# Loading the attention weights by casting transfers and issuing every second FFN weight load from ScalarE

## The reference, cut to what matters

```python
x = x + attn(layernorm(x), Wq, bq, Wk, bk, Wv, bv, Wo, bo)
# ffn, on layernorm(x):
h = silu(tlin(x, w1_w, w1_s)) * tlin(x, w2_w, w2_s)      # 1024 -> 4096
h = gelu(tlin(h, h1_w, h1_s))                            # 4096 -> 4096
h = gelu(tlin(h, h2_w, h2_s))                            # 4096 -> 4096
return x_mid + tlin(h, w3_w, w3_s)                       # 4096 -> 1024
```

## Time and profile before

| | us |
|---|---|
| median of 2 runs | 6946.5 (6782.0 and 7111.1) |
| the profiled execution | 6785.2 |
| its span, slowest core | 6783.7 |
| spans of the 8 cores | 6731.2 to 6783.7 |
| TensorE busy | 5790.8 (85%) |
| VectorE, ScalarE, GpSimd busy | 959.4, 658.8, 389.6 |
| end of the attention part | about 1370 |

### The profile page before, as it was taken

One profiled execution on the slowest core, in us unless ns is written; L12 is line 12 of the kernel. 1 busy time (PEld: TensorE's weight loads), 2 busy tenths in 40 slices (PEclk: granted clock), 3 DMA queues, 4 the chain that ended last, 5 costly groups with the idle time before them and its releaser, 6 DMA issues.

```text
span 6783.7 us, 75111 instructions; the slowest of 8 cores (6731.2 to 6783.7 us)
## 1 busy us (share of the span) xinstructions
PE 5790.8 (85%) x28409; PEld 2752.3 (41%) x28409; DVE 959.4 (14%) x2378; ACT 658.8 (10%) x1088; POOL 389.6 (6%) x625
## 2 busy tenths in 40 slices
PE   0355558969997999799979998999899989998998
PEld 0233335534443444344434443444344434443444
DVE  0343336620002000200020002000200020002000
ACT  0000000011001100110011001100100010001100
POOL 0000001100000000000000000000000000000000
PEclk9977779989998999999999999999999999999999
DMA  9999971034443444344434433444344334443443
GB/s 160 129 124 125 125 107 38 35 109 149 149 149 127 152 149 157 124 149 154 155 124 149 151 147 124 149 150 148 128 151 148 144 130 149 149 143 124 152 152 137
DMA packets 143589, 919.33 MB, mean 136 GB/s; under 512 B 16064, under 2 KB 16128, under 8 KB 65808
## 3 DMA queue, kind: packets, MB, share of 16 engines
q0 software_dynamic: 83488, 536.50, 30.8%
q1 hardware_dynamic: 59760, 378.04, 16.1%
HBM read 974.76 MB, written 126.35 MB: 162 GB/s over the span
## 4 chain that ended last, share of the span: by engine, by line
PE 73%; DMA 10%; another core or an unknown queue 7%; DVE 4%; issue 4%; ACT 1%; DVEq 0%; POOL 0%; POOLq 0%; ACTq 0%; SPq 0%
PE Z L892 50%; DMA p_w12r<-w12s 7%; PE Z L932 6%; PE Z L830 4%; PE Z L844 3%; PE Z L598 3%; PE Z L661 2%; PE Z L633 2%; DMA p_wbig<-h1s 1%; PE Z L549 1%; DMA p_wbig<-h2s 1%; PE Z L796 0%; PE Z L441 0%; DVE f_lnfm L800 0%
## 5 line engine op out<-in xcount | busy, mean ns | idle before, releaser
L892 PE MATMUL Z<-f_aT,p_wbig 128*128 128x512 bf16 x8192 | 1780.5, 379 | 13.4 <-DMA p_wbig<-h1s 6.5
L892 PE MATMUL Z<-f_bT,p_wbig 128*128 128x512 bf16 x8192 | 1779.6, 379 | 9.7 <-DMA p_wbig<-h2s 6.2
L892 PEld LDWEIGHTS Z<-f_aT,p_wbig 128*128 128x128 bf16 x8192 | 796.2, 98 | 996.4 <-issue 47.6
L892 PEld LDWEIGHTS Z<-f_bT,p_wbig 128*128 128x128 bf16 x8192 | 796.9, 98 | 991.1 <-issue 41.2
L830 PE MATMUL Z<-f_lnfm,p_w12r 128*128 128x512 bf16 x2048 | 494.4, 385 | 161.1 <-DMA p_w12r<-w12s 160.3
L947 DVE TENSOR_SCALAR f_o3T<-Z,p_s 128x512 f32<-128x512 f32 x64 | 48.1, 751 | 3981.8 <-PE Z L932 3981.8
L844 PE MATMUL Z<-f_lnfm,p_w12r 128*128 128x512 bf16 x2048 | 489.7, 382 | 6.2 <-DVE f_ost L965 6.2
L932 PE MATMUL Z<-f_aT,p_wbig 128*128 128x512 bf16 x2048 | 446.0, 379 | 5.1 <-DMA p_wbig<-w3s 2.7
L598 PE MATMUL Z<-a_lnfm,a_wq 128*128 128x256 bf16 (+1 forms) x1088 | 148.9, 306 | 287.2 <-DVE a_wot L557 285.0
L830 PEld LDWEIGHTS Z<-f_lnfm,p_w12r 128*128 128x128 bf16 x2048 | 193.1, 98 | 438.0 <-issue 233.8
L912 ACT ACTIVATE f_aT<-Z,p_sh 128x512 bf16<-128x512 f32 x256 | 176.0, 687 | 1612.0 <-PE Z L892 1612.0
(11 more groups left out here) (89 smaller groups left out, 2198.3 us busy)
## 6 DMA issues: line engine op xcount, KB each, us to landing
p_wbig<-h1s SPq DMA_DIRECT2D x128, 1024.0 KB, 4.8
p_wbig<-h1s POOLq DMA_DIRECT2D x128, 1024.0 KB, 6.1
p_wbig<-h2s SPq DMA_DIRECT2D x128, 1024.0 KB, 4.8
p_wbig<-h2s POOLq DMA_DIRECT2D x128, 1024.0 KB, 5.8
p_w12r<-w12s POOLq DMA_DIRECT2D x135, 512.0 KB, 3.7
p_w12r<-w12s SPq DMA_DIRECT2D x121, 512.0 KB, 3.2
h1s<-h1b POOLq DMA_DIRECT2D x8, 4096.0 KB, 194.6
h2s<-h2b POOLq DMA_DIRECT2D x8, 4096.0 KB, 114.2
```

The costliest lines, as they stand in the source:

```text
L892: N0=N0: e.matmul(zb[:, 0:N0], wbig[ws][:, ic * 128:ic * 128 + 128], src[:, ic * TPMAX:ic * TPMAX + N0], start=(ic == 0), stop=(ic == NHC ...
```

## The change

Two edits. First, Wk, Wv and Wo are loaded as Wq is, by casting transfers that GpSimd issues; the staging buffer, the six conversions and the waits on `stg_done` go away. Second, the FFN weight loads that GpSimd issued (odd chunks, and both of `w12_pref`) are issued by ScalarE, at the same place in the list and with the same waits on buffers; they count on SyncE's pool of semaphores.

```diff
@@ start @@
     cast_w("wq", wq_s)
+    cast_w("wk", wk_s)
+    cast_w("wv", wv_s)
     load_x(2)
     load_x(3)
-    stg = ar.al("a_stg", [128, 4096], F32, at=ar.offset_of(xmst[0]))
-    prev_conv = None
-    cvi = 0
-    for nm, dst in (("wk", wk_s), ("wv", wv_s), ("wo", wo_s)):
-        evs = []
-        for h in range(2):
-            ld = E("sy", lambda e, s=w_in[nm], h=h: e.dma_start(
-                out=stg[:], in_=s[:, h * 4096:(h + 1) * 4096]),
-                waits=[prev_conv], inc=sd, inc_by=16)
-            if cvi % 2 == 0:
-                cv = E("dv", ... e.tensor_copy(...), waits=[ld], inc=dv)
-            else:
-                cv = E("ac", ... e.copy(...), waits=[ld], inc=ac)
-            cvi += 1
-            prev_conv = cv
-            evs.append(cv)
-        wcast[nm] = tuple(evs)
-    stg_done = prev_conv
+    cast_w("wo", wo_s)
@@ wo_tile @@
-                       wotmp_free[u % 2] if oh == 0 else None,
-                       stg_done if (u <= 1 and oh == 0) else None], inc=dv)
+                       wotmp_free[u % 2] if oh == 0 else None], inc=dv)
...
-                   xmid_spill[u - 2] if u >= 2 else None,
-                   stg_done if u <= 1 else None], inc=po)
+                   xmid_spill[u - 2] if u >= 2 else None], inc=po)
@@ ffn_stage_a @@
-                w12_pref[(p, sl)] = E("gp", lambda e, sl=sl: e.dma_start(
+                w12_pref[(p, sl)] = E("ac", lambda e, sl=sl: e.dma_start(
                     out=w12r[sl][:], in_=w12s[sl]),
                     waits=[conv_ev[("w12", 0)], w12_free[sl]],
-                    inc=gd, inc_by=16)
+                    inc=sd, inc_by=16)
@@ ffn_pass, w12 chunks @@
-                eng, pool = ("sy", sd) if oc % 2 == 0 else ("gp", gd)
+                eng = "sy" if oc % 2 == 0 else "ac"
                 d1 = E(eng, lambda e, oc=oc, sl=sl1: e.dma_start(
                     out=w12r[sl][:], in_=w12s[oc]),
                     waits=[conv_ev[("w12", oc // 8)], w12_free[sl1]],
-                    inc=pool, inc_by=16)
+                    inc=sd, inc_by=16)
@@ ffn_pass, h1 and h2 chunks @@
-                eng, pool = ("sy", sd) if pc % 2 == 0 else ("gp", gd)
+                eng = "sy" if pc % 2 == 0 else "ac"
                 dd = E(eng, lambda e, pc=pc, hs=hsrc, ws=wslot: e.dma_start(
                     out=wbig[ws][:], in_=hs[pc]),
                     waits=[conv_ev[(hkey, pc // 4)], wbig_free[wslot]],
-                    inc=pool, inc_by=16)
+                    inc=sd, inc_by=16)
```

More of the change, by code:

```diff
@@ L289, in build_nc @@
     cast_w("wq", wq_s)
+    cast_w("wk", wk_s)
+    cast_w("wv", wv_s)
     load_x(2)
     load_x(3)
-    stg = ar.al("a_stg", [128, 4096], F32, at=ar.offset_of(xmst[0]))
-    prev_conv = None
-    cvi = 0
-    for nm, dst in (("wk", wk_s), ("wv", wv_s), ("wo", wo_s)):
-        evs = []
-        for h in range(2):
-            ld = E("sy", lambda e, s=w_in[nm], h=h: e.dma_start(
-                out=stg[:], in_=s[:, h * 4096:(h + 1) * 4096]),
-                waits=[prev_conv], inc=sd, inc_by=16)
-            if cvi % 2 == 0:
-                cv = E("dv", lambda e, d=dst, h=h: e.tensor_copy(
-                    d[:, h * 4096:(h + 1) * 4096], stg[:]),
-                    waits=[ld], inc=dv)
-            else:
-                cv = E("ac", lambda e, d=dst, h=h: e.copy(
-                    d[:, h * 4096:(h + 1) * 4096], stg[:]),
-                    waits=[ld], inc=ac)
-            cvi += 1
-            prev_conv = cv
-            evs.append(cv)
-        wcast[nm] = tuple(evs)
-    stg_done = prev_conv
+    cast_w("wo", wo_s)
     ld_ev = {}
```

## The result

The changed kernel took 9952.0 us as the median of 11 runs (9576.6 to 10133.9), the kernel before 6948.1 us as the median of 10. The profiled execution took 9581 us with a span of 9579.5, against 6785 and 6783.7 before: 2796 us more in the span.

The account below looks back on a forecast made before the run. Transfers were taken to bound the attention and TensorE's unbroken matmul chain the passes, so late odd loads would stall it. From 6785 us, start +16, w12 +257, h1 and h2 +2800 gave 9858, so 9860; range 8900 to 10,350.

Parts of the forecast that it names:

- h1 and h2: the waits: FFN stages h1 and h2: TensorE stalls 8.3 us for late weights at each of 256 odd chunks.
- h1 and h2: the clock behind them: After each of the 256 h1 and h2 stalls, TensorE's clock stays low, losing 2.6 us; 666 us in all.
- table loads in h1: First odd chunk of h1 in each pass: the load also stands behind a 1.28 us table load; 10 us.
- w12: waits, net: w12 stage: 121 stalls of 2.75 us each, less 136 us of present waits that go away.
- w12: clock: w12 stage: the clock falls after some of 121 stalls, taken as a third of 1.4 us, 0.5 each.
- w3: w3 stage: ScalarE has no evacuations there, so its loads wait only for buffers as before; price 0.
- start: Attention start: TensorE's 263.0 us wait goes without gain, as conversion transfers bound the groups; +16 us, bounds -10 and +30.
- No sharing: Rival for h1 and h2: ScalarE's load is served as if alone, stall 6.15 us, total 9308; 17%.
- The clock stays up: Rival for the FFN: TensorE's clock stays up or rises at once after stalls, total 9134; 8%.
- The loads hidden: Rival for the FFN: ScalarE issues loads once buffers are free, past the waiting evacuation, total 6716; 4%.
- The start pays: Rival for the attention: groups aren't bound by conversions, up to 240 us come back, total about 9620; 5%.

Follow-up runs that it names:

- the FFN loads alone: The kernel before with only the FFN loads of GpSimd moved to ScalarE, the start as before: 9598 us.
- the w12 stage alone: The kernel with the changed start, only w12's odd loads issued by ScalarE, h1, h2 and w3 loading as before: 7045 us.
- the filled stalls: The changed kernel with 32 further matmuls, results not read, ahead of each odd chunk of h1 and h2 from the third on: 9092 us.
- the start alone: The changed kernel with GpSimd issuing the odd FFN loads again, so only the start differs from before: 1.0007 of before, 6775 us profiled.
- Forcing it: The changed kernel with SyncE's load of each even chunk of h1 and h2 waiting for the odd chunk's load to land: 8936 us.
- the spread: The kernel before with its 22 conversions spread: none ahead of the groups, two in each of groups 0 to 5, one in 6 to 15: 6584 and 6598 us.

## Why the prediction was right, step by step

I had said 9860 us, within 8900 and 10,350; the profiled execution took 9581. The mechanism is the one that was predicted, at the predicted 256 places. The terms:

| term | predicted | measured |
|---|---|---|
| h1 and h2: the waits | 256 x 8.3 = 2125 | 1977 - 13 = 1964 |
| h1 and h2: the clock behind them | 256 x 2.6 = 666 | 554 |
| table loads in h1 | 10 | in the waits |
| w12: waits, net | +197 | +156 |
| w12: clock | 60 | 110 |
| w3 | 0 | 0.8 of waits, 2.7 before |
| start | +16 | about 0 |
| not assigned | | 12 |
| sum | 3075 | 2796 |

The clock's 554 is from the FFN loads alone and its 110 from the w12 stage alone, each by the busy time of the same matmuls. 554 makes 2.2 us for each stall, which the resumptions (2.1 to 2.2) and the filled stalls (2.2) give too.

*The stall, 8.3 for 7.7.* The place of the loads, their going out together, and the sharing were right. The second MB was mis-sized: I let it add 2.6 to 3.2 us, took 2.9 of it, and it adds 7.1 - 4.8 = 2.3. That is the whole difference. And I left open whether ScalarE issues while its Gelu runs; it does, 0.18 us after the start.

*The clock, 2.6 for 2.2.* It falls behind these stalls, as inferred: the mean over all 256 of them, 2.2 us, is what single ones cost. But I took the 5.3 us at the low level from resumptions after waits of some 30 us; after these stalls it was 4.2 to 4.4. The Trainium skill (TensorE: Matmul & The Clock Gate, HAM oscillation) describes a loop that starts each burst slow after a wait for a transfer; the trace agrees, with a mean of 421 ns for 379, and the run with the filled waits gained 489 us.

*w12, +257 for +266.* The sum is near, its parts less so, and that they made up for each other is luck. The waits were smaller: +156, between the +197 of my 2.75 us each and the +112 (248 - 136) of my lower value, 2.05, for an issue during the Silu. The clock fell more often than at a third of them: in one stretch of the changed kernel's trace, 3464 to 3556 us, there are ten such waits, of 1.8 to 3.9 us, and behind five of them the matmuls are slow (2.96 to 3.49 us for eight, where all eight have a record, against 1.89). The upper bound of 402 uses more than the 1.4 us of rows 10 for each low clock, and doesn't say from where.

*The start.* Right in its reason; its size is too small to be tested, as the ratio of the start alone, 1.0007, has an interval of -13 to +22 us, with both +16 and 0 in it. The casting loads were quicker than I had them: Wk landed at 35.0 us and Wv at 47.4, 12.4 us apart, under the 13 that I had as the lowest. By an estimate from that, the three cost 37 us for the 33 (an estimate too) removed.

*The rivals.* No sharing: fell, with landings of 7.1 us where one load alone takes 4.8. Forcing it gives 8936, below the 9308 that I had worked out: the stall is then 5.5 us and not 6.15, and the clock behind it costs 1.9 and not 2.6, together 1.3 us at 256 places. The clock stays up: fell. The loads hidden: not in the changed kernel, but it is what the same loads do at another place in the list, 6689 and 6687 us where I had 6716 for it. The Trainium skill (DMA: Bandwidth & Descriptors, Issuing engines are not separate DMA queues) says that transfers of all issuing engines run on the same 16 DMA engines and interleave. For the transfers themselves the runs agree: with ScalarE's loads ahead of the evacuation, and with SyncE's alone, times (6689 and 6687 us) and landings (4.9 us) are the same. What decides is what stands ahead of the load on the engine that issues it. The start pays: fell in this order, and is true, at 69 us, in another.

## What to carry to other kernels

Before a load is given to an engine that also computes, write out that engine's list and look at what the item ahead of the load waits for: the load can't go out before that. A double-buffered load behind the evacuation of the previous chunk is a load without a buffer; put on the list ahead of that evacuation it cost nothing here (6689 us, against 6687 from an engine without other work). And where TensorE waits for weights in every pair of chunks, count the low clock behind each wait as well, here 2.2 us for 7.7, over a quarter of the wait again. A wait that a change removes pays only if the next thing needed is there: ask what the engine will wait for instead.

## What the runs showed of the hardware that I had not expected

ScalarE issued a load 0.18 us after the start of a Gelu of 0.69 us that stood ahead of it in its list: here the computing instruction didn't have to end for the load to go out.

Two loads of 1 MB that start together land after 6.4 and 7.1 us, one alone after 4.8: the second MB took 2.3 us. That is some 450 GB/s by an estimate from these landings, more than in the fullest stretch that I had seen before (350).

The low clock after a stall of 7.7 us lasted 4.2 to 4.4 us, after waits of 31 to 38 us 4.4 to 5.8. With stalls of 5.5 us it cost 1.9 us each, not 2.2, so it was shorter again. In w12, waits near 2 us were followed by slow matmuls at some places and not at others. Why it differs wasn't tried.

The order of the conversions is worth more than the start edit: the spread took 178 us off the attention (1382 to 1204) with the same bytes. The traces fit this reason: groups bound by transfers and groups bound by compute had stood one behind the other. Before, the transfer engines are busy all the time only to some 900 us of the 6784, with TensorE busy half of it, and from 1050 to 1350 us about a tenth of the time, with TensorE busy nine tenths. With the spread both are busy from 600 to 1050 us: the transfer engines 0.78 to 0.98 of the time, TensorE 0.69 to 0.89.
